# A gated cross-attention and mixture-of-experts layer on one core: key transposes in a later group, weight splits in early rounds, table reads at the head of a step, and two semaphores for the two weights

## What is computed

```python
q, (k, v) = ln(x) @ Wq, split(ctx @ Wkv)
q, k = apply_axial_rope(q, pos), apply_axial_rope(k, pos)
attn = softmax(q @ k.T * scale) @ v
x = x + tanh(g_xattn) * (attn @ Wout + bout)
xf = ln(x)
shared_out = (silu(g) * u) @ shared_w2.T        # g, u = halves of xf @ shared_w1.T
routing_weights, selected = top_k(softmax(xf @ gate_w.T), 6)
gate_up = einsum('th,eoh->teo', xf, w1)
moe_out = einsum('te,tei,ehi->th', combine, silu(gate) * up, w2)
x = x + tanh(g_ffn) * (moe_out + shared_out)
```

## Time and profile before

| | |
|---|---|
| span of the profiled execution | 1807.0 us |
| its own time | 1808.88 us |
| median of three | 1808.34 us |
| busy PE, DVE, ACT, POOL | 1625.6, 738.4, 499.3, 670.7 us |
| phase A, barrier and first step of B, routed blocks, shared part | about 0 to 735, 735 to 767, 767 to 1575, 1575 to 1807 us |

### The profile page before, as it was taken

One profiled execution on the slowest core, in us unless ns is written; L12 is line 12 of the kernel. 1 busy time (PEld: TensorE's weight loads), 2 busy tenths in 40 slices (PEclk: granted clock), 3 DMA queues, 4 the chain that ended last, 5 costly groups with the idle time before them and its releaser, 6 DMA issues.

```text
span 1807.0 us, 32322 instructions
## 1 busy us (share of the span) xinstructions
PE 1625.6 (90%) x9026; PEld 1340.6 (74%) x9027; DVE 738.4 (41%) x1527; ACT 499.3 (28%) x986; POOL 670.7 (37%) x1135
## 2 busy tenths in 40 slices
PE   4999999999999992299999999999999999879998
PEld 2666666666666652188888888888888888869997
DVE  3556565565555554022222222222222222234555
ACT  3334333333333330022222222222222222211111
POOL 2224333333334336322633333333333330164342
PEclk8788777787877755599999999999999999989999
DMA  4002211111112214423333333333333332245563
GB/s 159 16 27 75 106 71 62 62 62 62 62 62 90 74 60 156 157 71 125 119 119 124 125 119 119 125 125 119 119 121 123 124 119 72 87 143 189 160 194 119
DMA packets 76310, 190.53 MB, mean 105 GB/s; under 512 B 10497, under 2 KB 12546, under 8 KB 73570
## 3 DMA queue, kind: packets, MB, share of 16 engines
q1 hardware_dynamic: 54562, 99.81, 17.3%
q0 software_dynamic: 21696, 90.06, 13.7%
HBM read 117.07 MB, written 72.76 MB: 105 GB/s over the span
## 4 chain that ended last, share of the span: by engine, by line
PE 46%; POOL 7%; DVE 3%; issue 2%; SPq 1%; ACT 0%; DMA 0%; DVEq 0%; POOLq 0%
PE bank L1306 27%; PE bank L1334 14%; POOL w_lo L219 3%; PE bank L1285 2%; PE bank L1315 2%; POOL w_lo L212 2%; POOL w_hi L208 2%; DVE tree L1394 1%; POOL w_hi L205 1%; DVE comb L1399 0%; DVE tree L1396 0%; SPq L1137 0%; DVE tree L1397 0%; DVE x_lo L1368 0%; SPq L1138 0%
## 5 line engine op out<-in xcount | busy, mean ns | idle before, releaser
L1306 PE MATMUL bank<-w_hi,x_hi 128*128 (+1 forms) x1152 | 294.1, 336 | 44.0 <-issue 25.3
L1306 PE MATMUL bank<-w_lo,x_hi 128*128 (+1 forms) x1152 | 279.8, 324 | 0.0
L1306 PE MATMUL bank<-w_hi,x_lo 128*128 (+1 forms) x1152 | 279.6, 324 | 0.0
L1306 PEld LDWEIGHTS bank<-w_hi,x_hi 128*128 128x128 f32 x1152 | 194.8, 189 | 70.4 <-issue 70.4
L205 POOL CAST w_hi<-w_raw 128x512 fp32r<-128x512 f32 (+1 forms) x54 | 31.0, 612 | 534.6 <-PE bank L1334 534.6
L1385 DVE SCALAR_TENSOR_TENSOR act<-silu,row_w,bank 128x352 f32<-128x352 f32 x112 | 65.0, 581 | 386.6 <-issue 199.5
L1257 ACT ACTIVATE silu<-bank 128x352 f32<-128x352 f32 x144 | 66.9, 464 | 530.2 <-PE bank L1306 530.2
L1306 PEld LDWEIGHTS bank<-w_lo,x_hi 128*128 128x128 f32 x1152 | 202.1, 189 | 0.0
L1306 PEld LDWEIGHTS bank<-w_hi,x_lo 128*128 128x128 f32 x1152 | 201.8, 189 | 0.0
L630 PE MATMUL bank<-k_t,q_t 32*128 32x256 f32 x512 | 197.6, 519 | 1.4 <-ACT k_t L579 1.4
L1334 PE MATMUL bank<-w_hi,a_hi 128*128 (+3 forms) x432 | 172.7, 400 | 2.2 <-DVE a_lo L1374 1.6
(11 more groups left out here) (184 smaller groups left out, 2612.8 us busy)
## 6 DMA issues: line engine op xcount, KB each, us to landing
xr<-expert_rows SPq DMA_DIRECT2D x112, 264.0 KB, 2.7
y_rows<-y SPq DMA_DIRECT2D x112, 256.0 KB, 2.0
w_raw<-in_w POOLq DMA_DIRECT2D x18, 1408.0 KB, 6.7
w_raw<-in_w POOLq DMA_DIRECT2D x18, 512.0 KB, 7.6
x_sb<-in_x SPq DMA_DIRECT2D x16, 256.0 KB, 3.0
x_res<-in_x SPq DMA_DIRECT2D x16, 256.0 KB, 4.1
x_rows<-x SPq DMA_DIRECT2D x16, 256.0 KB, 4.4
x_rows<-row SPq DMA_DIRECT2D x16, 256.0 KB, 4.5
```

The lines of the kernel that those rows point to most:

```text
L1306: last = nc.tensor.matmul(to[:, 0:WIDTH], xx[jt][:, d, :], w[d][half][:, cols], start=(d == 0 and xx is x_hi and w is w1_hi), stop=(d == D ...
```

## The change

1. PE's transposes of k move from u = 5 to u = 6. ACT's copy of q moves from the end of u = 4 to the head of u = 5, behind the copy of the transposed row; its two copies of k move from the end of u = 5 to the head of u = 7.
2. `split_w` becomes `split_w1` and `split_w2`. For experts 0 and 1 they run at the end of rounds 1 and 2, and 4 and 5; the load of the next expert follows each `split_w2`, so expert 2 is loaded in round 5.
3. In `phase_b` POOL splits w1 of expert e once `h_mm` frees its slot (the `up` of the last block of e - 2), then w2 once `y_mm` does. w1 comes first. `up` waits for `w1_made`, `down` for `w2_made`.
4. PE reads the table at the head of a step: the reads of `up` come ahead of the waits and products of `down`, and `down` reads the expert as well, for its new wait. Four reads in place of three.

```diff
+        def split_w1(pool, e):
+            s = slice(e % SLOTS * WIDTH, (e % SLOTS + 1) * WIDTH)
+            halves = [slice(0, WIDTH), slice(WIDTH, 2 * WIDTH)]
+            pool.wait_ge(w1_in, 16 * (e + 1))
+            for d in range(DC):
+                for half in range(2):
+                    nc.gpsimd.tensor_copy(w1_hi[d][half][:, s], w1_raw[:, d, halves[half]]).then_inc(w_hi_made, 1)
+            for d in range(DC):
+                pool.wait_ge(w_hi_made, 11 * e + 2 * d + 2)
+                for half in range(2):
+                    nc.gpsimd.tensor_tensor(w1_lo[d][half][:, s], w1_raw[:, d, halves[half]],
+                                            w1_hi[d][half][:, s].bitcast(F32), ALU.subtract).then_inc(w1_made, 1)
+        def split_w2(pool, e):
...
+            pool.wait_ge(w_hi_made, 11 * (e + 1))
             for c, (_, m) in enumerate(WC):
+                nc.gpsimd.tensor_tensor(w2_lo[c][0:m, s], w2_raw[0:m, c, :], w2_hi[c][0:m, s].bitcast(F32),
+                                        ALU.subtract).then_inc(w2_made, 1)
+        def load_after_split(pool, e):
+            pool.wait_ge(w1_made, 8 * e)
+            pool.wait_ge(w2_made, 3 * e)
+            load_w(nc.gpsimd, e)
...
+            def early_weights(r):
+                if r in (1, 4):
+                    split_w1(pool, r // 3)
+                if r in (2, 5):
+                    split_w2(pool, r // 3)
+                    load_after_split(pool, r // 3 + 1)
...
-                    if isinstance(at(PLACE)[0], int) and at(PLACE)[0] == BATCHES - 3:
-                        split_w(pool, 0)
-                        pool.wait_ge(w_made, 8)
-                        load_w(nc.gpsimd, 1)
-                    if isinstance(at(PLACE)[0], int) and at(PLACE)[0] == BATCHES - 1:
-                        split_w(pool, 1)
+                if at(LOAD) and isinstance(at(LOAD)[0], int):
+                    early_weights(at(LOAD)[0])
...
+                    if at(PROJECT) and u == 5:
+                        b, j, n = at(PROJECT)
+                        act.wait_ge(qt_mm, b + 1)
+                        need(act, score_mm, (b - 1) * GROUPS)
+                        a.activation(q_t[j][:].rearrange("p c n -> p (c n)"), bank[0][:], ACT.Copy)\
+                            .then_inc(qt_done, 1)
+                    if at(PROJECT) and u == 7:
...
+                        a.activation(k_t[j][:, :, 0, :], k4, ACT.Copy, scale=const[:, C_EVEN:C_EVEN + 1])\
+                            .then_inc(kt_done, 1)
                     attend(at, u)
...
-                if u == 5:
+                if u == 6:
                     pe.wait_ge(k_rope_done, b + 1)
                     pe.wait_ge(qt_done, b + 1)
                     four_transposes(bank[0], k_rope).then_inc(kt_mm, 1)
...
-                pool.wait_ge(w_made, 8 * e)
                 if e == 4:
                     find_rows_of_y()
-                load_w(nc.gpsimd, e)
-
                 last = BLOCKS if e == EXPERTS + SHARED - 1 else \
                     pool.value_load(ends_i[0:1, e - 2:e - 1], min_val=1, max_val=BLOCKS)
+                waits_apart(pool, passed_pool, (h_mm, last))
+                split_w1(pool, e)
                 waits_apart(pool, passed_pool, (y_mm, last))
-                split_w(pool, e)
+                split_w2(pool, e)
+                if e + 1 < EXPERTS + SHARED:
+                    load_after_split(pool, e + 1)
...
                     off = pe.value_load(table[0:1, bass.ds(g * T_N + T_W2, 1)], min_val=0, max_val=D)
+                    e = pe.value_load(table[0:1, bass.ds(g * T_N + T_EXPERT, 1)], min_val=0, max_val=EXPERTS - 1)
+                    ready = 3 * (e + 1)
                     cols = bass.ds(off, D)
...
+                w1_block = w1_at(i, at)
                 pe.wait_ge(a_lo_done, g + 1)
+                pe.wait_ge(w2_made, ready)
...
-                if live(i, -2):
-                    down(i, at)
+                w1_block = down(i, at) if live(i, -2) else w1_at(i, at)
...
                 if live(i, 0):
-                    up(i, at)
+                    up(i, at, *w1_block)
```

More of the change, by code:

```diff
@@ L203, in split_w @@
+        def split_w2(pool, e):
+            s = slice(e % SLOTS * D, (e % SLOTS + 1) * D)
             pool.wait_ge(w2_in, 32 * (e + 1))
             for c, (_, m) in enumerate(WC):
[L205 to L209, removed]
+                nc.gpsimd.tensor_copy(w2_hi[c][0:m, s], w2_raw[0:m, c, :]).then_inc(w_hi_made, 1)
@@ L542, in one_round @@
                             .then_inc(at_hi_done, 1)
+                    if at(PROJECT) and u == 5:
[5 more added lines that the diff above has]
+                    if at(PROJECT) and u == 7:
+                        b, j, n = at(PROJECT)
+                        act.wait_ge(kt_mm, b + 1)
+                        need(act, score_mm, (b - 1) * GROUPS)
+                        k4 = bank[0][:].rearrange("p (c n) -> p c n", c=DC)
+                        a.activation(k_t[j][:, :, 0, :], k4, ACT.Copy, scale=const[:, C_EVEN:C_EVEN + 1])\
+                            .then_inc(kt_done, 1)
+                        a.activation(k_t[j][:, :, 1, :], k4, ACT.Copy, scale=const[:, C_ODD:C_ODD + 1])\
+                            .then_inc(kt_done, 1)
                     attend(at, u)
@@ L565, in one_round @@
                                          ACT.Copy).then_inc(v_done, 1)
[L566 to L570, removed]
-                        if u == 5:
-                            act.wait_ge(kt_mm, b + 1)
-                            need(act, score_mm, (b - 1) * GROUPS)
-                            k4 = bank[0][:].rearrange("p (c n) -> p c n", c=DC)
-                            a.activation(k_t[j][:, :, 0, :], k4, ACT.Copy, scale=const[:, C_EVEN:C_EVEN + 1])\
-                                .then_inc(kt_done, 1)
-                            a.activation(k_t[j][:, :, 1, :], k4, ACT.Copy, scale=const[:, C_ODD:C_ODD + 1])\
-                                .then_inc(kt_done, 1)
                     if at(LOAD) and isinstance(at(LOAD)[0], int) and at(LOAD)[0] == 0 and u == 5:
@@ L1286, in transpose_x, with w1_at, up @@
                 last.then_inc(x_mm, 1)
-            def up(i, at):
+            def w1_at(i, at):
+                if live(i, 0) and routed(i, 0):
+                    g = at(0)[0]
+                    e = pe.value_load(table[0:1, bass.ds(g * T_N + T_EXPERT, 1)], min_val=0, max_val=EXPERTS - 1)
+                    off = pe.value_load(table[0:1, bass.ds(g * T_N + T_W1, 1)], min_val=0, max_val=WIDTH)
+                    return 8 * (e + 1), bass.ds(off, WIDTH)
+                if live(i, 0):
+                    s = (i - BLOCKS) % SHARED
+                    return 8 * (EXPERTS + s + 1), slice(s * WIDTH, (s + 1) * WIDTH)
+            def up(i, at, ready, cols):
                 g, j, n = at(0)
                 t, jt, nt = tile(i, at, 0)
-                if routed(i, 0):
-                    e = pe.value_load(table[0:1, bass.ds(g * T_N + T_EXPERT, 1)], min_val=0, max_val=EXPERTS - 1)
-                    ready = 8 * (e + 1)
-                    off = pe.value_load(table[0:1, bass.ds(g * T_N + T_W1, 1)], min_val=0, max_val=WIDTH)
-                    cols = bass.ds(off, WIDTH)
-                else:
-                    ready = 8 * (EXPERTS + (i - BLOCKS) % SHARED + 1)
-                    s = (i - BLOCKS) % SHARED
-                    cols = slice(s * WIDTH, (s + 1) * WIDTH)
                 pe.wait_ge(x_lo_done, t + 1)
                 need(pe, act_done, g)
-                pe.wait_ge(w_made, ready)
+                pe.wait_ge(w1_made, ready)
                 for d in range(DC):
@@ L1337, in down @@
                 last.then_inc(y_mm, 1)
+                return w1_block
             pe.wait_ge(table_in, 16)
```

25 lines of the change are left out of this document (6 added, 19 removed).

## The result

The changed kernel takes 1877.47 us (median of four executions, 1859.82 to 1878.39), the kernel before 1808.2 on the same chip: 1.0364 times the time, 95% interval 1.0301 to 1.0426. It is 3.6% slower where 3% faster was forecast, and lies outside the range. The profiled execution took 1877.71 us, with a span of 1875.8, which is 68.8 more than before.

The account below looks back on a forecast made before the run. PE was taken to set the pace in nearly all loop rounds and routed steps. Terms +4 - 27 - 11 - 16 - 6 + 2 = -54 from 1808.88, less 0.54, gave 1754 us, range 1733 to 1780.

Parts of the forecast that it names:

- k transposes: Phase A rounds: moving them uncovers 0.88 us behind the row, mostly absorbed; +4 us, bounds +12 and -27.
- about 2.5 us: Phase A: PE would wait this long for DVE's row in 14 rounds, with no wait left for q.
- a pair may absorb it: Phase A: alternating unequal rounds may absorb the added work, so +4 us was taken instead of +12.
- The bound +12: Phase A: upper bound for the k transposes' move, 14 rounds times 0.88 us uncovered behind the row.
- Rival A: Phase A: the pause falls otherwise and full clock lasts 4.6 us longer on average; 1722 us, chance 0.10.
- Table reads: Routed steps: reads at the step's head are covered, giving back 0.26 us in 104 steps; -27 us, bound +70.
- It should come to the reads that much earlier: Routed steps: the sequencer issues `up` about 1.5 us earlier, so it reaches the next reads earlier and they are covered.
- At least 0.93 us: Routed steps: the price of three more reads ahead of `down`, besides one more wait.
- Rival D: Routed steps: the sequencer is the bound, each of 104 steps 0.93 us longer than forecast; 1851 us, chance 0.04.
- Passage to the shared part: Phase B: `up` of weights 17 starts 13.4 us earlier, late gathers cost 3.8; -11 us, bounds -15 and -7.
- Splits out of the late rounds: End of phase A: expert 1's split gone gives -16 us, expert 0's in round 17 gives -6.
- Early splits: Early phase A rounds: POOL's splits may hold DVE's L948 and L954; +2 us, bounds 0 and +13.

Follow-up runs that it names:

- extra8: Kernel before with eight useless transposes of row ahead of the real ones in every round: 1821.87 us, ratio 1.0002.
- pause: Kernel before with ACT copying q_t three times instead of once, no PE work added: 1869.59 us, ratio 1.0256.
- k_less3: Kernel before with the k transposes one group later and three of the twelve q projection products left out: 1830.71 us, ratio 1.0061.
- reads_only: Kernel before with its three table reads of a step all ahead of `down`, no fourth read or second wait: 1787.29 us, ratio 0.9833.
- reads_mid: Changed kernel with the two reads of `up` moved between the products of `down` and the activation's transposes: 1775.37 us, ratio 0.9726.
- best: Kernel before with splits moved (expert 0 rounds 1 and 2, expert 1 round 16), `up` awaiting both weights, its reads mid-step: 1736.16 us, ratio 0.9544.
- splits_only: Changed kernel without the k transposes' move and with the reads of `up` back just ahead of `up`: 1790.39 us, ratio 0.9861.
- b_fill: Kernel before with 16 useless identity transposes in PE's pause between the q and k transposes: 1792.36 us, ratio 0.9880.
- best_fill: Kernel with the paying parts together, plus 16 useless identity transposes in PE's q_t pause, against the kernel before: 1705.74 us, ratio 0.9360.
- extra4: Kernel before with four useless transposes of row ahead of the real ones in every round: 1821.76 us, ratio 1.0007.
- k_fill: Kernel before with the k transposes one group later and 16 useless identity transposes ahead of the wait for row: 1824.26 us, ratio 1.0016.
- k_only: Kernel before with only the k transposes one group later and ACT's copies moved as in the change: 1854.10 us, ratio 1.0142.

## Why the prediction was wrong

**k transposes** (+4 forecast, about +37): the reading of the timeline held. The wait for row took q's place, "about 2.5 us" came out as 2.48, and 0.88 was the wait for the exponential. (Two readings of the earlier trace rows were loose: POOL's root ends at 501.31 and not 501.6, and DVE is idle for 2.22 us of it only. Neither changes the sum.) What failed is the step from there to time: "a pair may absorb it". I had summed work moved behind the row, and took the idle time as unchanged since q's 27.2 us only changed its name. But PE's idle time in that place rose from 1.95 (2.9 in every second round) to 3.36 us, since the k transposes no longer stood between the waits. Pauses and work aren't priced alike in this loop: 2 us of work cost nothing (extra8), 1.3 us more in one pause cost 3.4 a round (pause). That isn't a rule for every arrangement, as k_less3 shows. The bound +12 was too low by a factor of three, because it multiplied 0.88 by a count of rounds. Rival A had the right lever, the pause, with the wrong sign. Its 18.5 us at half clock were a window's length; the stretch of that round is almost 24, the mean of the pair 20.5.

**Table reads** (-27 forecast, +54 in after): two steps failed. "It should come to the reads that much earlier": its lead over PE is 2.4 us at the first read, and that is less than four reads take. "At least 0.93 us" for three reads was the bare TENSOR_LOAD; with the register work a read costs 0.77, so four take 3.1 of the 3.4 us, and the waits come on top. Three reads at the head (reads_only) are hidden for the greater part; it took the fourth, with its wait, to make the step slower than before. Rival D named the mechanism, with 0.93 us a step above the forecast and slower "from 0.52"; the step came out 0.77 above the forecast 6.98, and I had given D a chance of 0.04. The Trainium skill ("TensorE: Matmul & The Clock Gate", table at its head) gives a queue of 64 entries, from which I had concluded that the reads are covered. The trace does not contradict the number but the conclusion: at the first read, 2.4 us at 0.16 us a product are some 15 products, and with their loads 30 entries, were ahead of PE.

The prize was mis-sized too. I took the 0.26 us of PE's own row; a row of before that I had not used tells the true one:

```profile
PEld bank L1306 <- issue: 70.4, 113, 15.6
```

Less the one wait of 15.6 that is 54.8 / 112 = 0.49 us a step. A matmul's record reaches beyond the start of its successor (0.48 us for two that start 0.16 apart), so PE's row hides a part of each gap. 7.24 - 0.49 = 6.75 is within 0.01 of what reads_mid and best take, and after's 7.75 less its 112.2 / 109 = 1.03 of PEld gives 6.72.

**Passage to the shared part** (-11, measured -9.3): `up` of weights 17 is 13.3 us nearer, forecast 13.4; from there to the end 4.0 are given back, where 3.8 for the gathers less 1.7 for a shorter `up` were forecast. DVE's first `tree` does wait for its gather, 4.10 us.

**Splits out of the late rounds** (-16 and -6): -16.0 at the memset, exactly; L963 takes at most 236 ns, and PE's wait for attn, 7.65 us in the earlier trace rows, is 0.9.

**Early splits** (+2, bounds 0 and 13): the hold is real, but the instruction was another. xn waits 9.97 us from 151.09 while POOL's L205 and L209 run from 150.23 to 160.77, and PE stands 4.2 us for it. I had looked at instructions with two inputs in SBUF only. The Trainium skill ("SBUF - State Buffer", Who interferes with whom) also names `tensor_scalar` among the operations that can, in some modes, contend for the port pair shared with GpSimd, and the held instructions of after and splits_only are both of that kind; on this the trace agrees. By the same section of the Trainium skill the side that issues first has the pair for its whole instruction. The trace shows more than that: each hold spans a whole run of POOL instructions (9.97 us against 0.89 for one subtraction), although POOL's stream has semaphore waits between them. In sum with the late rounds splits_only shows +1.2 at the scatter where -4 was forecast.

**Sum.** -54 forecast; +68.8 measured: +37 in place of +4, +54 in place of -27, and some 9 us of small misses. The chances were too sure: D and the k move's price were both bounded by rows of the wrong kind.

## What to carry to other kernels

Where the clock alternates inside a loop, price idle time and work of PE apart, and try a filler of useless matmuls in the longest pause before reordering real work around it. Table reads belong where the sequencer waits for another engine anyway; count them at their spacing, not at the length of the load, and read PEld's issue time, not PE's. A long run of POOL instructions is to be placed behind a wait for the last DVE instruction at that place that reads and writes SBUF, as the three held ones here do.

## What was not expected of the hardware

- The mean round is near one of three values: 37.98 (b_fill, best_fill), 40.95 (before, extra4, extra8, and others), 44.36 (after, reads_mid, pause), 3.0 and 3.4 us apart, while the work differs by up to 2 us among kernels of the same value. Kernels between them (k_fill, k_less3) have irregular rounds. Why these values, the experiments don't show. Nor is a kernel bound to one of them: one execution of after took 1859.8 us with a mean granted clock of 0.883, the other three 1877.2 to 1878.4 with 0.872 to 0.874.
- After a fall the clock stays at half for some 10 us (b_fill), 17 or 24 (before) or 27 us (after, k_only, pause); 27 us in round after round belongs to kernels that idle over 3 us around the fall, but k_less3 idles as long and has it only now and then.
- Four table reads a step cost nothing in two pairs (6.74 us), and 1.0 us a step in a row (7.75).
- A `tensor_scalar` of 16 columns (0.23 us) was held 7.86 us by POOL.
